# First aggregation: deeper one-hot and weight buffers, one head's weights on VectorE, sums of weights kept in PSUM

## The reference

```python
xp = (x @ W).reshape(N, H, C)            # N 3125, H 4 heads, C 256
e = leaky_relu(a_src[src] + a_dst[dst])  # self-loops are appended to the edges
ee = exp(e - segment_max(e, dst)[dst])
z = segment_sum(ee, dst)
out = segment_sum(xp[src] * (ee / z[dst])[:, :, None], dst)
```

## Time and profile before

| | us |
|---|---|
| median of the runs (lowest, highest) | 2171.18 (2164.91, 2173.71) |
| span of the profiled execution | 2761.9 |
| first aggregation in the profiled execution | 780 to 1494 |

### The profile page before, as it was taken

One profiled execution on the slowest core, in us unless ns is written; L12 is line 12 of the kernel. 1 busy time (PEld: TensorE's weight loads), 2 busy tenths in 40 slices (PEclk: granted clock), 3 DMA queues, 4 the chain that ended last, 5 costly groups with the idle time before them and its releaser, 6 DMA issues. The chain is left out here.

```text
span 2761.9 us, 52467 instructions
## 1 busy us (share of the span) xinstructions
PE 1865.4 (68%) x11779; PEld 1216.8 (44%) x11780; DVE 1524.7 (55%) x4081; ACT 862.2 (31%) x2923; POOL 1346.7 (49%) x1446
## 2 busy tenths in 40 slices
PE   5612119999857777777774886367677676856678
PEld 4300004444434555545553775244445444545544
DVE  5301006777655555555555996254544544678878
ACT  3000000000246666656564674100000000046656
POOL 1576770000046666666663112826666666147781
PEclk9855558999979999999998998688888888979999
DMA  8201002332168888888887994556766666478857
GB/s 302 49 2 21 4 15 72 98 91 87 44 203 297 295 291 291 291 292 295 291 293 239 306 308 145 145 154 193 192 194 190 194 194 195 141 218 310 308 187 267
DMA packets 256917, 531.76 MB, mean 193 GB/s; under 512 B 50253, under 2 KB 148694, under 8 KB 256782
## 3 DMA queue, kind: packets, MB, share of 16 engines
q0 software_dynamic: 95376, 276.01, 32.0%
q1 hardware_dynamic: 124142, 220.58, 23.8%
q10 hardware_dynamic: 37296, 33.96, 5.0%
HBM read 441.14 MB, written 102.23 MB: 197 GB/s over the span
## 5 line engine op out<-in xcount | busy, mean ns | idle before, releaser
L165 POOL DMA_INDIRECT acc<-xl_table,csrc x392 | 401.3, 1024 | 243.7 <-issue 110.7
L1274 ACT ACTIVATE wone<-onehot,w 128x64 f32<-128x64 f32 x1760 | 433.3, 333 | 278.3 <-DVE onehot L1320 174.0
L1291 PE MATMUL banks<-w_sb,wone 128*64 128x256 f32 x2368 | 346.6, 416 | 135.1 <-DVE acc L1316 42.1
L990 PE MATMUL banks<-w_sb,acc 128*128 128x512 f32 x736 | 367.1, 637 | 36.7 <-issue 36.5
L1768 PE MATMUL banks<-xr_parts,onehot_t 128*128 x1320 | 228.3, 314 | 241.3 <-issue 186.4
L165 POOL DMA_INDIRECT w_sb<-xp_table,isrc x296 | 294.5, 995 | 171.8 <-PE banks L1294 91.5
L1808 DVE SCALAR_TENSOR_TENSOR prod<-banks,att_relu 128x1024 f32<-128x1024 f32 x110 | 134.6, 1223 | 323.2 <-ACT w L1727 238.2
L1316 DVE TENSOR_TENSOR acc<-banks,acc 128x512 f32 x440 | 304.4, 692 | 0.0
L1768 PEld LDWEIGHTS banks<-xr_parts,onehot_t 128*128 128x128 bf16 x1320 | 137.3, 104 | 343.7 <-issue 302.3
L165 POOL DMA_INDIRECT ga<-a_src_table,csrc x240 | 239.4, 998 | 94.9 <-issue 76.6
L1291 PEld LDWEIGHTS banks<-w_sb,wone 128*64 128x64 f32 x2368 | 183.1, 145 | 193.5 <-issue 83.2
(11 more groups left out here) (336 smaller groups left out, 2966.0 us busy)
## 6 DMA issues: line engine op xcount, KB each, us to landing
edge_rows<-acc SPq DMA_DIRECT2D x440, 130.0 KB
rows<-edge_rows SPq DMA_DIRECT2D x55, 1040.0 KB, 5.0
lt_bc<-local_dst ACTq DMA_DIRECT2D x110, 128.0 KB
lt<-local_dst ACTq DMA_DIRECT2D x110, 128.0 KB
w<-acc SPq DMA_DIRECT2D x100, 128.0 KB, 3.4
x_table<-y POOLq DMA_DIRECT2D x25, 512.0 KB, 6.2
acc<-x_table SPq DMA_DIRECT2D x25, 512.0 KB, 3.7
acc<-in_x SPq DMA_DIRECT2D x12, 1024.0 KB, 14.7
```

Source lines behind the costliest of these rows:

```text
L165: return self.pool.indirect_dma_start(out, None, table, bass.IndirectOffsetOnAxis(ap=idx, axis=0), bounds_check=self.bound, oob_is_err=False)
L990: last = nc.tensor.matmul(psum[:, 2 * r + i], xT_all[:, u, k, :], w_sb[:, k, i * 512:(i + 1) * 512], start=(k == 0), stop=(k == KD - 1))
L1274: last = nc.scalar.activation(wone[:, s, j, h, :], onehot[:, s, j, :], ACT.Copy, scale=w9[:, bass.ds(g * U + j, 1), h:h + 1].rearrange("p ...
L1291: nc.tensor.matmul(psum[WN * a:WN * (a + 1), j, k * C:(k + 1) * C], wone[:, s, j, h, :], slots[r][:, j, h * C:(h + 1) * C], start=True, st ...
```

## The change

The four lookup tensors (`ga`, `nt0`, `as0`, `chi`) get their own scope, closed ahead of the first aggregation. The room goes to a third buffer of `onehot` and `wone`. Then:

- DVE runs two stages a turn: `build` of group g, then `add` of group g-2. `build` makes the one-hots and, after a wait for them, multiplies them with head 0's weights of all four steps in one instruction. The additions into `zacc` are gone; the `acc` additions stay. The waits for the stored projections stand ahead of the first build, and the clearing of the third row buffer moves from the build of group 0 to that of group 1.
- ACT makes heads 1 to 3 only, 12 instructions a group, with one wait a group.
- PE uses six banks (0 to 5) in turn, so that it waits for the add of six steps back. The 9 sums of weights are accumulated in bank 7 at the column of the step's window: PE reads the group's four window numbers into registers, multiplies each by 9, and gives the product as the address. Two matmuls of 450 columns with the cleared `zacc` open and close the bank. DVE copies it to `zacc` at the end.
- All three loops have bodies of 3 groups. POOL's loop, the 12 slots and the gathers stay as they are.

```diff
+        lookups = top.enter_context(ExitStack())
...
+        lookups.close()
         with ExitStack() as ph:
             def sb(name, shape, dt=F32):
                 return ph.enter_context(nc.sbuf_tensor(name, shape, dt))
+            BUFS = 3
+            BANKS = 6
+            assert 3 * U % BANKS == 0
             rows_c = sb("rows0_c", [P, 1, U, D])
             slots = [rows[:, 0], rows[:, 1], rows_c[:, 0]]
-            onehot = sb("onehot0", [P, 2, U, WN])
-            wone = sb("wone", [P, 2, U, H, WN])
+            onehot = sb("onehot0", [P, BUFS, U, WN])
+            wone = sb("wone", [P, BUFS, U, H, WN])
             accw = acc[:].rearrange("p t (w n) -> p (t w) n", w=2)
             s_o = sem("p2_o")
             s_pa = sem("p2_pa")
             s_mm = sem("p2_mm")
             s_acc = sem("p2_acc")
+
+            WEIGHTS = 7
+            assert BANKS <= WEIGHTS and NWP * W9 <= 512
             with nc.Block() as block:
                 @block.gpsimd
                 def _(pool):
-                    nc.gpsimd.memset(acc[:, NU:NT, :], 0.0).then_inc(s_zero, 1)
+                    nc.gpsimd.memset(acc[:, NU:NT, :], 0.0).then_inc(s_cleared, 1)
                     gather = PoolGather(pool, N, bound)
                     for i in range(2):
                         gather.wait(s_xs[i], 16 * ((NT - 1) // 2))
...
 
                 @block.scalar
                 def _(act):
-                    def weights(g, s, m):
-                        s = s % 2
-                        act.wait_ge(s_o, g + 1)
+                    def weights(g, r, m):
+                        act.wait_ge(s_o, 2 * g + 2)
                         for j in range(U):
-                            wait(act, s_mm, (g - 2) * U + j + 1)
-                            for h in range(H):
-                                last = nc.scalar.activation(wone[:, s, j, h, :], onehot[:, s, j, :], ACT.Copy,
+                            for h in range(1, H):
+                                last = nc.scalar.activation(wone[:, r, j, h, :], onehot[:, r, j, :], ACT.Copy,
                                                             scale=w9[:, bass.ds(g * U + j, 1), h:h + 1].rearrange("p a b -> p (a b)"))
                             last.then_inc(s_pa, 1)
-                    pipelined(act, NG, [(0, weights)], 6, 6)
+                    pipelined(act, NG, [(0, weights)], 3, 3)
 
                 @block.tensor
                 def _(pe):
-                    def group(g, s, m):
-                        r, m3, s = s % 3, 2 * m + s // 3, s % 2
+                    windows = StepTiles(pe, wtab, "p2_w", U, NW)
+                    column = [pe.alloc_register(f"p2_column{j}") for j in range(U)]
+
+                    def group(g, r, m):
+                        windows.load(g)
+                        for j in range(U):
+                            pe.reg_alu(column[j], windows.regs[j], W9, ALU.mult)
+                        columns = [pe.snap(c, min_val=0, max_val=(NW - 1) * W9) for c in column]
                         for j in range(U):
                             i = g * U + j
-                            pe.wait_ge(s_r[r][j], 16 * m3 + 16)
+                            bank = (r * U + j) % BANKS
+                            pe.wait_ge(s_r[r][j], 16 * m + 16)
                             pe.wait_ge(s_pa, i + 1)
-                            wait(pe, s_acc, i - 3)
+                            wait(pe, s_acc, i - BANKS + 1)
                             for k in range(2):
                                 for a in range(2):
                                     h = 2 * a + k
-                                    nc.tensor.matmul(psum[WN * a:WN * (a + 1), j, k * C:(k + 1) * C],
-                                                     wone[:, s, j, h, :], slots[r][:, j, h * C:(h + 1) * C],
+                                    nc.tensor.matmul(psum[WN * a:WN * (a + 1), bank, k * C:(k + 1) * C],
+                                                     wone[:, r, j, h, :], slots[r][:, j, h * C:(h + 1) * C],
                                                      start=True, stop=True)
-                            nc.tensor.matmul(psum[0:WN, 4 + j, 0:W9], onehot[:, s, j, :],
+                            nc.tensor.matmul(psum[0:WN, WEIGHTS, bass.ds(columns[j], W9)], onehot[:, r, j, :],
                                              w9[:, bass.ds(i, 1), :].rearrange("p a n -> p (a n)"),
-                                             start=True, stop=True).then_inc(s_mm, 1)
-                    pipelined(pe, NG, [(0, group)], 6, 6)
+                                             start=False, stop=False).then_inc(s_mm, 1)
+
+                    def add_zeros(start, stop):
+                        return nc.tensor.matmul(psum[0:WN, WEIGHTS, 0:NWP * W9], ident[:, 0:WN],
+                                                zacc[:].rearrange("p t n -> p (t n)"), start=start, stop=stop)
+                    add_zeros(True, False)
+                    pipelined(pe, NG, [(0, group)], 3, 3)
+                    add_zeros(False, True).then_inc(s_mm, 1)
 
                 @block.vector
                 def _(dve):
                     tiles = StepTiles(dve, wtab, "p2", U, NW)
 
-                    def group(g, s, m, build=True, add=True):
-                        if add:
-                            ds = tiles.load(g - 1)
+                    def build(g, r, m):
+                        wait(dve, s_mm, (g - BUFS + 1) * U)
+                        nc.vector.tensor_tensor(
+                            onehot[:, r], bc(iotar[:, 0:WN].unsqueeze(1), [P, U, WN]),
+                            bc(wdst[:, bass.ds(g * U, U)].unsqueeze(2), [P, U, WN]), ALU.is_equal).then_inc(s_o, 1)
+                        dve.wait_ge(s_o, 2 * g + 1)
+                        nc.vector.tensor_tensor(
+                            wone[:, r, :, 0, :], onehot[:, r],
+                            bc(w9[:, bass.ds(g * U, U), 0:1], [P, U, WN]), ALU.mult).then_inc(s_o, 1)
                         if isinstance(g, int) and g == 1:
-                            dve.wait_ge(s_zero, 1)
+                            nc.vector.memset(rows_c[:], 0.0).then_inc(s_clr, 1)
+
+                    def add(g, r, m):
+                        ds = tiles.load(g)
+                        if isinstance(g, int) and g == 0:
+                            dve.wait_ge(s_cleared, 1)
                         for j in range(U):
-                            if add:
-                                i = (g - 1) * U + j
-                                dve.wait_ge(s_mm, i + 1)
-                                wait(dve, s_acc, i)
-                                av = accw[:, bass.ds(ds[j], 1), :].rearrange("p a n -> p (a n)")
-                                zv = zacc[0:WN, bass.ds(ds[j], 1), :].rearrange("p a n -> p (a n)")
-                                nc.vector.tensor_tensor(zv, psum[0:WN, 4 + j, 0:W9], zv, ALU.add)
-                                nc.vector.tensor_tensor(av, psum[:, j, :], av, ALU.add).then_inc(s_acc, 1)
-                            if build and j == 0:
-                                wait(dve, s_mm, (g - 1) * U)
-                                wait(dve, s_pa, (g - 1) * U)
-                                nc.vector.tensor_tensor(
-                                    onehot[:, s], bc(iotar[:, 0:WN].unsqueeze(1), [P, U, WN]),
-                                    bc(wdst[:, bass.ds(g * U, U)].unsqueeze(2), [P, U, WN]), ALU.is_equal).then_inc(s_o, 1)
-                                if isinstance(g, int) and g == 0:
-                                    for i in range(2):
-                                        dve.wait_ge(s_xs[i], 16 * ((NT - 1) // 2))
-                                    dve.wait_ge(s_last_xp, 32)
-                                    nc.vector.memset(rows_c[:], 0.0).then_inc(s_clr, 1)
-                    pipelined(dve, NG, [(0, lambda g, s, m: group(g, s, m, True, not (isinstance(g, int) and g == 0)))], unroll=2)
-                    group(NG, 0, NG // 2, False, True)
+                            i = g * U + j
+                            bank = (r * U + j) % BANKS
+                            dve.wait_ge(s_mm, i + 1)
+                            wait(dve, s_acc, i)
+                            av = accw[:, bass.ds(ds[j], 1), :].rearrange("p a n -> p (a n)")
+                            nc.vector.tensor_tensor(av, psum[:, bank, :], av, ALU.add).then_inc(s_acc, 1)
+                    for i in range(2):
+                        dve.wait_ge(s_xs[i], 16 * ((NT - 1) // 2))
+                    dve.wait_ge(s_last_xp, 32)
+                    pipelined(dve, NG, [(0, build), (2, add)], 3, 3)
+                    dve.wait_ge(s_mm, T + 1)
+                    nc.vector.tensor_copy(zacc[0:WN].rearrange("p t n -> p (t n)"), psum[0:WN, WEIGHTS, 0:NWP * W9])
```

10 lines of the change are left out of this document (5 added, 5 removed).

## The result

The changed kernel takes 2176.28 us (median of 7 runs, 2173.82 to 2177.39), the kernel before 2170.13 beside it (7 runs, 2164.91 to 2173.71). The ratio is 1.0029, interval 1.0019 to 1.004: 6.3 us slower, where 21 faster was forecast. The size lies within the 0.5% called no change, but the sign is clear.

The account below looks back on a forecast made before the run. Late PE signals in a ring through one-hots and weights were taken to hold the gathers; 2.8 + 606 + 13.0 + 1.4 = 623 us against 644 gave 21 less, 2150 us, range 2130 to 2165.

Parts of the forecast that it names:

- the timed stage: First aggregation, 714 us in the profiled execution; estimated at 644 in the timed runs by taking off 70 for late signals.
- the other stages: Logits' stage and second layer's loop: profiled excess missing from timed runs, up to 296 and 217 us, some 495 together.
- Rival 2: First aggregation already at the gathers' pace in timed runs: 619 us before, 619 to 623 after; 2165 to 2175; chance 0.29.
- the clearing: Clearing of the third row buffer at the aggregation's start, 3.47 us, ending before POOL's ninth gather needs it: cost nothing.
- rival 4: First aggregation: a build's second instruction holds POOL up, 0.42 us each; stage 656, +12, time 2183; chance 0.04.
- The ring: First aggregation: PE's late signal, DVE's addition, one-hots, ACT's weights, PE's next group; 7.1 us, mean 6.34, removed by the change.
- The pace: Time per gather step in the changed first aggregation: 1.38 us, the 1.324 from the bytes plus 4%, over 439 steps.
- ACT, DVE, PE: Work per group in the first aggregation: ACT 2.95 us, DVE 4.65, PE 4.3 to 5.0, all hidden below 5.3.
- Start: First aggregation up to its first gather: 2.8 us, with the new wait and the moved buffer clearing adding nothing.
- End: First aggregation after the last gather: 13.0 us as before, plus 1.4 for the closing matmul and the copy.

Follow-up runs that it names:

- prompt trace: Second trace of the unchanged kernel, nothing changed, on a chip where it takes about 2170 us; measured 2169.27 us, span 2167.6.
- earlier trace: First profiled execution of the unchanged kernel, the one the prediction was read from, chip not known; it took 2761.9 us.

## Why the prediction was wrong

The step that failed is the size of the timed stage: "I give it 70 (bounds: 30 and 95). By this estimate the timed stage takes 714 - 70 = 644 us." It takes 582, which is 132 less. The 594.3 us between the two traces of the unchanged kernel divide into 283.9 before the first gather (I had up to 296), 128.4 between first and last gather (70), and 182.1 behind (up to 217). I took nearly the largest possible share for the other stages, 495 where they have 466, and of the 95 that this left gave the stage 70, little over half of the 128; even the upper bound of 95 was too low. So the wait that the change was to remove (a ring of one-hots, weights and additions that holds the gathers) is not in the timed runs at all: they stand at POOL's own pace already. Rival 2 had this mechanism, with a chance of 0.29, but not its numbers: it put the stage at 619 before and the time at 2165 to 2175, and that the time would rise it gave 0.02. The rise comes from a term at "nothing", the clearing, and from rival 4.

- *The ring.* Rival 2 made it 3.6 us with prompt signals. With the 1.28 of the prompt trace and the other pieces of the earlier trace rows (0.74, 0.56 and 1.19) it is 3.8, an estimate, below 5.18 as well. Nor is the depth of the ring what costs 0.26 a step in an execution like the first trace: on a slower chip, with three buffers, the pace is 1.609 for 1.588. So the forecast of 714 to 623 fails there too. PE's stops stand in the trace of that slower chip; what lies behind them is open.
- *The pace.* 1.38 was taken, 1.316 was measured, and 1.296 without the change. The lower bound of 1.324 from the bytes was not a bound: 352 GB/s of the earlier trace rows isn't the most the gathers reach (360 in the kernel with the clearing first and all heads by ACT), and half the bytes gain nothing. The 4% on top for unevenness were wrong: with the slots three deep nothing is lost beside the held gathers.
- *ACT, DVE, PE.* On prompt chips the product takes 0.425 (0.42 taken), additions stand 0.90 apart (0.89), ACT makes 12 instructions a group. All of it hidden, as said. PE's register work and the accumulation at a register's column cost nothing that shows: the kernel with the sums in PSUM alone stands at 1.0006.
- *Start.* The 2.8 to the first gather counts from 781; from the stage's edge at 780 it is 3.75, a slip of 1 us that decides nothing. "Nothing" for the clearing was wrong. The clearing was moved behind two builds, from 0.70 before the first gather to 0.91 behind its start, and cost 3.2 us, half of the loss (3.9 by the medians). The working looked at when the clearing ends, not at what its start meets.
- *End.* +1.4 was taken, about 0 measured: the last addition ends 7.65 behind the last gather, for 8.20 in the prompt trace of before, and the copy of 0.62 takes that back. The end of the changed kernel, for the earlier trace rows:
```profile
1082.21 0.95 PE L1312 MATMUL banks<-zacc,ident 128*64 128x450 f32 x2
1082.50 0.69 DVE L1344 TENSOR_TENSOR acc<-banks,acc 128x512 f32 x1 [0.29 <-PE banks L1307]
1083.19 0.62 DVE L1350 COPY zacc<-banks 64x450 f32<-64x450 f32 x1
1084.07 1.17 SPq L1432 DMA_DIRECT2D w<-acc  x2
```
- *Rival 4* had the mechanism and a price too high: 0.42 for each product. The 36 held gathers of the loop make 5.6 us, the one-hots' own holds among them, 0.05 a group. Only an instruction that starts in the gap between gathers holds one, and then by 0.12 in the mean. The row it was argued from, one gather of 1.232 in the earlier trace rows, was such a case, and not so rare: that trace has 15 gathers over 1.05, all behind a one-hot in the gap. The change doubles the number of instructions that can do it. The Trainium skill (SBUF, State Buffer, "Who interferes with whom") has a VectorE instruction with two inputs in SBUF contend with GpSimd's reading; the traces agree for the builds against the additions (36 held gathers behind builds, none behind the 154 additions that start in the gap in the changed kernel); the clearing, which reads nothing and held a gather too, is outside that rule. The traces add that it depends on where in the gather's cycle the instruction starts.

## To carry to other kernels

Where a profiled execution is a quarter longer than the timed runs, guessing each stage's share of the excess is not safe: here it was 128 us for one stage where 30 to 95 had been allowed. Price a stage for the timed runs at the pace that its issuing engine shows between stops (here 1.295, the median of the intervals, which was in the trace all along: 439 of them with the 2.8 and 13.0 around make 584, and the stage of the prompt trace is 582). An edit that adds or moves VectorE instructions beside a stream of indirect gathers should be asked where they fall in the gathers' cycle. Short ones hold less than a long one of the same work. A clearing belongs ahead of the first gather, not among them.

## What the runs showed of the hardware

- An indirect gather of 128 rows is issued each 1.295 us, 0.99 of it busy, for rows of 4 KB, and no faster for rows of 2 KB (1.305, 1.00 busy). With 4 KB 360 GB/s are reached.
- A VectorE instruction with its inputs in SBUF that starts in the 0.30 us between two gathers holds the second until 0.86 to 0.87 behind its own end: two-tensor builds of 0.42 by up to 0.26, a per-partition scalar product of 0.25 by 0.025 at the same overlap as 0.027 for the builds. 1316 additions of 0.69 with one input from PSUM held none.
- A VectorE clearing of 128x4096, with no input, that runs for 3.47 us held a gather for 3.2 and 3.6 us when it started in the gap before it or 0.03 ahead of the first, and did nothing when it started 0.70 ahead. So "two inputs in SBUF" is not the whole rule.
- Of 220 two-input instructions 47 fell into the gap in one kernel and 106 in another that differs in banks and in the sums of weights: a loop can lock to the gathers at a good or a bad point. In the traces this moved the held time of the loop between 0.5 us (unchanged kernel) and 8.6 (four banks).
- The experiments ran on three chips with the unchanged kernel at 2169 to 2170 us and on two with 2779 and 2788 (medians); on the latter PE loses its pace every 129 to 149 recorded instructions in this stage, PE's work before it runs late (105 us of 358 in the stage of the logits, for 355), and the mean granted clock is 0.85 to 0.87 for 0.96.
